# Loading the query operands of an attention unit in one 72-row transfer instead of three

## What is computed

```python
h = _layernorm(x) * (1 + ca) + sa
x = x + ga * _L0_attn_ref(h, Wk, bk, Wv, bv, Wf, bf)     # 16 heads of 8; Q is h itself; causal softmax
h = _layernorm(x) * (1 + cb) + sb
x = x + gb * _L0_ffn_ref(h, ...)                         # shared expert + 8 routed experts, top 2
...                                                      # layer 1, modulated in the same way:
x = x + ga * _L1_attn_ref(h, qkv_w, proj_w, proj_b, curvature)   # 6 plain, 4 hyperbolic, 6 cosine heads
x = x + gb * _L1_ffn_ref(h, ...)                         # shared expert + 16 gated experts, top 4
```

## Time and profile before

| | |
|---|---|
| time, median of 3 runs | 2967.86 us (2966.98 to 2972.3) |
| time of the profiled execution | 2972.27 us |
| its span, from first to last instruction | 2970.3 us |
| busy: TensorE, VectorE, ScalarE, GpSimd | 78%, 55%, 47%, 21% |
| DMA packets of all queues | 67750, 128.32 MB, 43 GB/s in the mean |

### The profile page before, as it was taken

The page is one execution under the profiler, slowest core; times in us unless marked ns, Lnnn a source line. Parts: engine busy times, 40 slices in busy tenths (PEclk is TensorE's granted clock), DMA queues, the critical chain, the costliest instruction groups (busy, mean ns, idle before and its releaser), DMA issues. The chain is left out here.

```text
span 2970.3 us, 30177 instructions
## 1 busy us (share of the span) xinstructions
PE 2308.0 (78%) x10649; PEld 862.5 (29%) x10649; DVE 1630.4 (55%) x3477; ACT 1392.6 (47%) x2011; POOL 631.4 (21%) x590
## 2 busy tenths in 40 slices
PE   3798857777999884777798986677779988577779
PEld 1232322223433341122342233122333223212134
DVE  2553446677456354675655536467655534466662
ACT  1145315893134531787224442389612453158932
POOL 1012102331311200332231120033223121013324
PEclk9599866678999885787899987578789998567789
DMA  5100220001400022000320013110041002200003
GB/s 140 40 18 2 72 71 29 17 1 56 124 20 17 16 68 75 30 2 1 106 85 24 2 40 78 40 31 1 11 128 53 18 1 72 71 29 17 1 33 89
DMA packets 67750, 128.32 MB, mean 43 GB/s; under 512 B 11300, under 2 KB 24740, under 8 KB 62980
## 3 DMA queue, kind: packets, MB, share of 16 engines
q1 hardware_dynamic: 67600, 126.40, 14.8%
HBM read 109.99 MB, written 15.20 MB: 42 GB/s over the span
## 5 line engine op out<-in xcount | busy, mean ns | idle before, releaser
L1281 DVE TENSOR_REDUCE mx<-ps 128x1 f32<-128x512 f32 (+3 forms) x1248 | 644.1, 553 | 562.1 <-PE ps L626 466.1
L1010 ACT ACTIVATE pr<-ps 128x1024 f32<-128x1024 f32 (+3 forms) x672 | 516.2, 805 | 544.8 <-PE ps L696 542.7
L623 PE MATMUL ps<-kop,qop 72*128 72x512 bf16 (+6 forms) x1248 | 438.9, 371 | 154.2 <-DVE mx L1281 88.1
L696 PE MATMUL ps<-qop,kop 75*128 75x512 bf16 (+7 forms) x1344 | 411.7, 371 | 164.0 <-DMA kop<-parts_scratch 57.7
L742 PE MATMUL ps<-pr,vt 128*32 128x512 f32 (+3 forms) x2688 | 445.0, 592 | 5.5 <-POOL pr L1544 4.9
L1544 POOL TENSOR_SCALAR_AFFINE_SELECT pr<-pr 128x512 f32<-128x512 f32 x224 | 148.4, 663 | 1159.2 <-ACT pr L1010 1157.6
L1065 ACT ACTIVATE pr<-ps 128x512 f32<-128x512 f32 x224 | 133.8, 598 | 400.9 <-PE ps L848 313.4
L623 PEld LDWEIGHTS ps<-kop,qop 72*128 72x128 bf16 (+1 forms) x1248 | 124.2, 101 | 609.2 <-DVE mx L1281 339.0
L858 PE MATMUL ps<-pr,w_down 128*128 128x512 f32 x384 | 209.9, 633 | 67.3 <-POOL pr L1535 46.2
L696 PEld LDWEIGHTS ps<-qop,kop 75*128 75x128 bf16 (+1 forms) x1344 | 123.4, 105 | 383.1 <-ACT pr L1010 125.8
L845 PE MATMUL ps<-hT,w_gate 128*128 128x512 f32 x384 | 207.3, 623 | 10.4 <-DVE on L1484 10.3
(11 more groups left out here) (286 smaller groups left out, 3046.2 us busy)
## 6 DMA issues: line engine op xcount, KB each, us to landing
wb<-gates_scratch SPq DMA_DIRECT2D x192, 256.0 KB, 3.4
qop<-parts_scratch SPq DMA_DIRECT2D x96, 192.0 KB
kop<-parts_scratch SPq DMA_DIRECT2D x96, 192.0 KB
on<-hmax_scratch SPq DMA_DIRECT2D x8, 1024.0 KB, 5.4
parts_scratch<-on SPq DMA_DIRECT2D x24, 256.0 KB, 4.1
parts_scratch<-wb SPq DMA_DIRECT2D x24, 256.0 KB, 2.9
xin<-in_x SPq DMA_DIRECT2D x4, 512.0 KB, 5.1
on<-in_cos SPq DMA_DIRECT2D x4, 512.0 KB, 3.8
```

Source lines behind the costliest of these rows:

```text
L623: mm = pe.matmul(o, qop[0:k, slot(l, u), j, qb * P:(qb + 1) * P], kop[0:k, slot(l, u), j, k0:k0 + wd], start=True, stop=not diag)
L696: mm = pe.matmul(o, kop[0:k, slot(l, u), 2 * pair + j, kb * P:(kb + 1) * P], qop[0:k, slot(l, u), 2 * pair + j, q0:q0 + wd], start=True, s ...
L1010: nc.scalar.activation(pr[:, g % 3, 2 * pair:2 * pair + 2, o0:o0 + wd], ps[:, bank:bank + 2, o0:o0 + wd], ACT.Exp).then_inc(a.exps, 1)
L1281: ins_ = nc.vector.tensor_reduce(mx[:, nth(l, u) % 2, j, qb, col % 2:col % 2 + 1], ps[:, bank, 0:wd], AX.X, ALU.max, negate=True)
```

## The change

The three loads of a unit's query rows become one: the same 24 rows of DRAM are read three times through a source of outer dimension 3 with stride 0, into 72 partitions. The three key loads stay. In layer 1 the query loads of units 0 and 3 now stand ahead of the stores of the key parts. In the layer-0 guest the loads of units 1 and 2 stand behind gate rows 6, 9, 12 and 15, a tile's whole load at a time. And ScalarE copies a gate tile at the end of the item before, ahead of the guest's value copy.

```diff
-OPS = 16 * 6
+OPS = 16 * 4
...
                 for i, (kind, e, c) in enumerate(f.work):
-                    if i in f.gates_at:
-                        n = f.gates_at.index(i)
-                        act.wait_ge(g.gps, n + 1)
-                        nc.scalar.copy(gT[0:E, n, :], ps[0:E, 7, :]).then_inc(g.gates, 1)
...
+                    if i + 1 in f.gates_at:
+                        n = f.gates_at.index(i + 1)
+                        act.wait_ge(g.gps, n + 1)
+                        nc.scalar.copy(gT[0:E, n, :], ps[0:E, 7, :]).then_inc(g.gates, 1)
                     guest.until(i)
...
-            def load_rows(l, u, side, i):
-
-                op = (qop, kop)[side]
+            def load_side(l, u, side):
+
                 heads = scratch[l, side, :, :, 4 * u:4 * u + 4, :].rearrange("i d h n -> i d (h n)")
                 if side:
-                    src = heads[i:i + 1].broadcast_to([3, HD, 4 * N])
+                    for i in range(3):
+                        sp.dma_start(kop[24 * i:24 * i + 24, slot(l, u), :, :].rearrange("p h n -> p (h n)"),
+                                     heads[i:i + 1].broadcast_to([3, HD, 4 * N])).then_inc(at[l].ops[u], 16)
                 else:
-                    src = heads.rearrange("i d n -> (i d) n")
-                sp.dma_start(op[24 * i:24 * i + 24, slot(l, u), :, :].rearrange("p h n -> p (h n)"),
-                             src).then_inc(at[l].ops[u], 16)
+                    rows = heads.rearrange("i d n -> (i d) n").unsqueeze(0)
+                    sp.dma_start(qop[0:PAIRS, slot(l, u), :, :].rearrange("p h n -> p (h n)"),
+                                 rows.broadcast_to([3, 3 * HD, 4 * N])).then_inc(at[l].ops[u], 16)
...
-                load_unit(0, 0)
-                for n in range(12):
-                    yield LOADS_FROM + n
-                    load_rows(0, 1 + n // 6, n // 3 % 2, n % 3)
+                for side in range(2):
+                    sp.wait_ge(at[0].stored[side], 48)
+                    load_side(0, 0, side)
+                for n in range(4):
+                    yield LOADS_FROM + 3 * n
+                    load_side(0, 1 + n // 2, n % 2)
...
-            for side in range(2):
-                store_parts(1, side, 3 * side, parts[:, side])
-            for u in (0, HYP_UNIT, 1):
-                load_unit(1, u)
+            store_parts(1, 0, 0, parts[:, 0])
+            sp.wait_ge(at[1].stored[0], 48)
+            for u in (0, HYP_UNIT):
+                load_side(1, u, 0)
+            store_parts(1, 1, 3, parts[:, 1])
+            sp.wait_ge(at[1].stored[1], 48)
+            for u in (0, HYP_UNIT):
+                load_side(1, u, 1)
+            load_hyp_rows(1, HYP_UNIT)
+            load_unit(1, 1)
```

More of the change, by code:

```diff
@@ L1587, in sync_program, with load_hyp_rows @@
         def sync_program(sp, b):
-            def load_rows(l, u, side, i):
-                op = (qop, kop)[side]
+            def load_side(l, u, side):
                 heads = scratch[l, side, :, :, 4 * u:4 * u + 4, :].rearrange("i d h n -> i d (h n)")
                 if side:
-                    src = heads[i:i + 1].broadcast_to([3, HD, 4 * N])
-                else:
-                    src = heads.rearrange("i d n -> (i d) n")
-                sp.dma_start(op[24 * i:24 * i + 24, slot(l, u), :, :].rearrange("p h n -> p (h n)"),
-                             src).then_inc(at[l].ops[u], 16)
+                    for i in range(3):
+                        sp.dma_start(kop[24 * i:24 * i + 24, slot(l, u), :, :].rearrange("p h n -> p (h n)"),
+                                     heads[i:i + 1].broadcast_to([3, HD, 4 * N])).then_inc(at[l].ops[u], 16)
+                else:
+                    rows = heads.rearrange("i d n -> (i d) n").unsqueeze(0)
+                    sp.dma_start(qop[0:PAIRS, slot(l, u), :, :].rearrange("p h n -> p (h n)"),
+                                 rows.broadcast_to([3, 3 * HD, 4 * N])).then_inc(at[l].ops[u], 16)
             def load_unit(l, u):
+                for side in range(2):
+                    load_side(l, u, side)
+            def load_hyp_rows(l, u):
                 a = at[l]
-                for side in range(2):
[L1603 to L1606, removed]
                 if is_hyp(l, u):
```

## The result

The changed kernel takes 3008.86 us (median of 4 runs, 2997.3 to 3012.01), the kernel before 2970.08 (4 runs, 2966.98 to 2976.1): a ratio of 1.0116, 95% interval 1.0093 to 1.014. The change costs some 34 us by the ratio and between the two profiled executions, 39 us by the medians. The forecast was 2982 us and slower: the sign is right, but the time lies 5 us above the range of 2961 to 3004.

The account below looks back on a forecast made before the run. No single engine fills the span; waits count, notably TensorE's for unit loads, whose key loads run on three engines. Terms 13 − 1 − 1 + 3 = +14 us on the 2967.9 median gave 2982 us, range 2961 to 3004.

Parts of the forecast that it names:

- That the new query load runs on three engines: Unit loads: the repeated-source query load uses three engines, 7.7 us at 77 GB/s; a unit's traffic 15.3 us instead of 11.5.
- rival 1: Query load spreads over 12 engines or more; key loads of layer 1 go out at 407.6: −48, 2920 us, chance 0.06.
- rival 5: Neither step shows: query loads as fast as now, the swapped gates' copy without effect; 2968 us, chance 0.04.
- Layer-1 unit 2: Unit load in layer 1, four times: 3.8 us more traffic exposed on PE, 3.2 us each, +13 us; bounds +8 and +15.2.
- Start of layer 1: Four times: early query loads hold up key stores, key loads issued about 417.3; −0.3 us each, −1 us; bounds −5 to +2.
- rival 2: Start of layer 1: key stores not held up by query loads ahead; −4.3 four times, 2966 us, chance 0.09.
- First unit: Layer-0 unit 0, once: with the engines to itself its load takes 16.8 us instead of 17.6, −1 us.
- The feed-forward with a guest: Layer 1, three times: early gates gain, three-engine backlog gives it back; +1 us each, +3; bounds −5.9 to +5.
- The early gates: Layer-1 feed-forward with a guest: the swapped copies bring gates, gate rows 0 to 3 and unit-0 loads 5.9 us forward.
- rival 3: Early gates carry through: all 5.9 us kept in three feed-forwards, −18 instead of +3, 2961 us, chance 0.08.
- Rival 4: Three engines overrun in the feed-forward: +5 three times, +2 per layer-1 start, full 15.2 for unit 2; 3005 us, chance 0.15.

Follow-up runs that it names:

- experiment 6: The changed kernel with query parts stored three times in DRAM, so the one 72-row query load repeats nothing: 2948.09 us, ratio 0.9949 to the kernel before.
- experiment 2: The changed kernel with three 24-row query loads in place of the 72-row one, order and copies kept: 2922.05 us, ratio 0.9838 to the kernel before.
- Experiment 9: The changed kernel with the guest's last block of key loads behind gate row 18 and the second gates' store: 2990.71 us, ratio 1.0087 to the kernel before.
- experiment 3: The kernel before with only the gates' copy moved in ACT's program: 2940.39 us, ratio 0.9883 to the kernel before.
- experiment 5: The changed kernel with three 24-row query loads in layer 0, layer 1 keeping the 72-row load: 2970.26 us, ratio 1.0017 to the kernel before.
- experiment 7: The changed kernel with three 24-row query loads and reordered key blocks, read by five loads without repeated source: 2877.72 us, ratio 0.9698 to the kernel before.

## Why the prediction was right in sign and wrong in size

| us | forecast | measured |
|---|---|---|
| layer 1, four (start and unit 2) | −1 + 13 | +25.4 |
| up to the first layer 1 | −1 | +1.1 |
| feed-forward with guest, three | +3 | +19.5 |
| layer 0 in between | no term | −11.9 |
| sum | +14 | +34.1 |

The direction and the mechanism, three engines, were right. Two terms of the sum were far too small, the feed-forward most of all, and a difference for which there was no term hid part of the error.

**That the new query load runs on three engines**: right, shown by the share of 0.19 and by experiment 6. So rival 1 falls for this form, and rival 5 with it. Rival 1's picture can be read from experiment 2, where the queries do spread: 2922, as it said, but in part by luck. The key loads go at 16.9 us and the hyperbolic unit is read at 39.4, four us earlier than before and not nine. Of the 50 us between the two profiled executions 23 lie in layer 1, 20 in the three feed-forwards, where the gates come early, and 8 in layer 0.

**Layer-1 unit 2** (+3.2 us each): the mechanism held, the size was off. It took 19.0 us, not 16.8: the traffic 16.0 instead of 15.3, the lead 1.9 from the issue at 536.65 to 538.6 instead of 0.5, and some 1.1 behind the last packet. The lead was read too short even for the old load, whose first packets come 0.9 us behind the issue; the new form's come at 1.9 here and near 1.55 in the other sequences. PE waits 5.1 to 6.1 us more, above the upper bound of 3.8 that I gave the traffic.

**Start of layer 1** (−0.3 us each): the hold-up of the key stores was right, and rival 2 falls. That its size was right to 0.3 us (26.1 against 25.8) is in part luck: the query loads' traffic ended 23.7 us behind the first store and not 22.4, and from there to the key loads it took 2.4 us and not 3.4. But the key loads have the long lead as well, once nothing runs ahead of them in their queues (first packets 1.5 us behind their issue): unit 0 is read 11.2 us behind it, not 9.2, and the hyperbolic unit 46.05 us behind the first store, 2.5 later than before (2.1 in the mean of the four sequences). With unit 2, layer 1 costs 25 us, where I had +12.

**First unit** (−1): its query load was issued at 68.47 and PE read it at 86.58, 18.1 us against 17.6 before; the units behind it still crowd in. The stretch up to layer 1 is 1.1 us longer.

**The feed-forward with a guest** (+1 us each): this is the step that failed by most. The forecast was that the three engines would be free in time for the second gates' rows, so that the early gates would nearly pay for the traffic; they weren't. Its first half was right. Against the first layer-0 store the gates and the first unit's loads came some 6 us earlier, product 4 2.7 us (I had said 2 to 5). The second half said that the three engines would be busy for 53.5 us and the second gates' rows then late by less than 3.6 us. They were busy from 739.9 to some 799 in the mean, 59 us, and product 16 came at 99.0 us against 91.6 before, 7.4 us late; two of the three feed-forwards grew by 7.3. Experiment 9 shows that this backlog, ahead of the gates' store, is what made the feed-forwards longer than before: with one block moved behind that store product 16 is in time and they take 143.8 us in the mean. The early gates are used up by the blocks ahead of it. The trace's records of single packets show where the 5.5 us more went. The 432 packets of the three units, 8 KB each, take 151.7 us of engine time, 50.6 us on each of the three engines, where I had 45.9. Half of that excess is there without any gate row, since the 144 packets of layer-1 unit 2 alone take 16.1 us on each engine and not 15.3; the other half comes only beside gate rows, and how it arises isn't shown. What is left, some 8 us, went to the gate rows' own packets (I had 7.6). Measured +7.3, +5.0 and +7.3, where I took +1 with +5 as the bound.

**The early gates**, which I held to be worth at most 5.9 us, are worth 8.7 where nothing uses them up (experiment 3). In the change nothing of them is left, so rival 3 falls. The two halves of the feed-forward term were each too small: the gain, and what the three-engine loads take from it, some 13 us (38 us in three, experiment 5 against the change) to 15 us (8.7 gained, 6.5 lost).

**Layer 0 in between** had no term. It was 12 us shorter, with a higher granted clock in two stretches of three; whether by the change or by chance isn't shown. The stages that the change touches cost 46 us. What sets the clock in layer 0 was not tried.

Rival 4 was nearest: 3005, with its +5 in the feed-forward, +2 at the start of layer 1, and the full 3.8 at unit 2. In the mean +6.5, +2.1 and +5.7 were measured, and the 12 us in layer 0 make up for two terms that are still too small; that its total came so near is luck. It had 0.15, and the stated range ended 1 us below it; the evidence for it, the 17.1 us from loads to gate row 4, was in the trace.

## What to carry to other kernels

Before merging loads, look at the outer dimension of both sides. Here three loads that spread over twelve engines beat one load that runs on three, and everything behind it in those queues waited too, stores that nobody thinks of included. Where such loads share a queue with small urgent rows, sum the backlog at the moment each urgent row is issued, and put the urgent store ahead of the last block. And when a form is read off another load's rows, read its lead off the same rows: here a load's first microseconds belonged to its form as much as its rate did.

## What the runs showed of the hardware

- A load with a repeated source on three engines has its first packets about 1.5 us behind the issue when nothing runs ahead of it: 1.51 us for the key loads at 418.67, 1.55 us for those at 409.82 in experiment 2 (share 0.07 for 410 to 412), 1.55 us for the 72-row load at 738.34; the one at 536.65, with 1.94 us (share 0.00 for 536.5 to 538.5), is the longest. With the same 72 rows not repeated it is 0.90 us (experiment 6, 538.11), and for the key loads of experiment 7 0.89 us (400.48).
- SP needs 0.69 to 0.77 us in the median to issue a load with a repeated source, of 24 rows or of 72, and 0.31 to 0.37 us for one without, of 72 rows too.
- The key-part stores took up to 13.2 us to land behind two loads on three engines, against 3.3 before.
- Unit-load packets of 8 KB took 0.335 us of engine time in the mean with nothing beside them (unit 2 of layer 1) and 0.351 us among gate rows (feed-forward at b = 1).
